# Two dense layers of a graph network in fp32: normalising a tile behind the product, the residual sum on VectorE, and the third layer's first transposes ahead of the second's last products

## What is computed

```python
h = (1.0 + eps) * node_feats + aggr                      # acc, 10 tiles of 128x512
h = gelu(layer_norm(h @ W1 + b1, g1, be1))               # W1 512x1024, layer 1
h = gelu(layer_norm(h @ W2 + b2, g2, be2))               # W2 1024x512, layer 2
h = layer_norm(node_feats + h, gA, bA)                   # layer A
m = gelu(h @ M1) @ M2                                    # M1 512x1024, M2 1024x512
return x + layer_norm(h + m, gB, bB)                     # layer B
```

## Time and profile before

| | before |
|---|---|
| median of 3 runs | 560.19 us (559.36 to 563.92) |
| the profiled execution | 567.65 us, of which span 565.8 us |
| busy share of the span: PE, DVE, ACT, POOL | 84%, 72%, 53%, 57% |
| chain that ended last: PE, DVE, issue, ACT, POOL | 43%, 23%, 15%, 7%, 6% |
| edges, W1, W2, M1 with M2 begin at about | 0, 302, 371, 443 us |

### The profile page before, as it was taken

How to read it: one execution, slowest core, us unless ns; L and a number is a source line. 1 busy time by engine, 2 the same in 40 slices (tenths; PEclk the granted TensorE clock), 3 DMA queues, 4 the chain that set the end, 5 groups by cost and what they waited for, 6 DMA issues and landing times.

```text
span 565.8 us, 7924 instructions
## 1 busy us (share of the span) xinstructions
PE 476.6 (84%) x1915; PEld 351.2 (62%) x1916; DVE 407.6 (72%) x550; ACT 300.2 (53%) x569; POOL 325.2 (57%) x306
## 2 busy tenths in 40 slices
PE   1072999977989897998868999999999699999994
PEld 0041666643656564665546887778877589888883
DVE  7861999872968686878891788878999844572465
ACT  3741786871876776878881444456554466004000
POOL 4675788875788787878730444426777542240152
PEclk9997799996989898999987999999999799999998
DMA  7676677776667676679306422343442031121022
GB/s 277 236 229 204 173 216 216 216 215 191 194 193 218 195 222 198 209 217 321 112 1 206 167 74 74 131 149 107 149 149 72 8 93 57 38 74 39 20 93 74
DMA packets 34296, 85.26 MB, mean 151 GB/s; under 512 B 4912, under 2 KB 5248, under 8 KB 34240
## 3 DMA queue, kind: packets, MB, share of 16 engines
q0 software_dynamic: 12560, 41.17, 25.1%
q1 hardware_dynamic: 20864, 42.74, 22.4%
q10 hardware_dynamic: 816, 0.77, 0.5%
HBM read 72.07 MB, written 5.24 MB: 137 GB/s over the span
## 4 chain that ended last, share of the span: by engine, by line
PE 43%; DVE 23%; issue 15%; ACT 7%; POOL 6%; ACTq 2%; DMA 2%; another core or an unknown queue 1%; DVEq 1%; POOLq 0%
PE ps_t L1154 7%; PE ps_u L1128 5%; PE ps_u L1138 5%; PE ps_u L1129 5%; PE ps_u L1130 5%; DVE work L1021 5%; PE ps_t L1130 4%; PE ps_t L1128 4%; PE ps_t L1129 4%; DVE msg_lo L952 3%; DVE z L947 3%; POOL rstd L533 3%; POOL rows L520 2%; ACT squares L754 2%; PE ps_t L1138 2%
## 5 line engine op out<-in xcount | busy, mean ns | idle before, releaser
L520 POOL DMA_INDIRECT rows<-gather_table,src_idx x157 | 191.1, 1217 | 61.5 <-issue 43.3
L696 ACT ACTIVATE msg_hi<-z 128x1024 fp32r<-128x1024 f32 (+1 forms) x79 | 82.7, 1047 | 61.0 <-DVE z L947 43.0
L952 DVE SCALAR_TENSOR_TENSOR msg_lo<-z,msg_hi 128x1024 fp32r<-128x1024 f32 (+1 forms) x79 | 100.9, 1279 | 0.7 <-ACT msg_hi L696 0.7
L1138 PE MATMUL ps_u<-we_raw,attr_raw 128*128 128x512 f32 x104 | 58.9, 651 | 42.3 <-DVE attr_lo L958 38.6
L947 DVE TENSOR_TENSOR z<-ps_u,rows 128x1024 f32<-128x1024 f32 (+1 forms) x53 | 64.1, 1210 | 38.9 <-remote 18.2
L531 POOL TENSOR_TENSOR var_eps<-mv,eps_t 128x1 f32<-128x1 f32 x40 | 11.5, 287 | 135.9 <-DVE mv L1009 68.3
L1128 PE MATMUL ps_u<-w_hi,lhs_lo 128*128 128x512 f32 x160 | 65.9, 412 | 4.2 <-DVE lhs_lo L1000 3.0
L1130 PE MATMUL ps_u<-w_hi,lhs_hi 128*128 128x512 f32 x160 | 63.8, 399 | 0.0
L1129 PE MATMUL ps_u<-w_lo,lhs_hi 128*128 128x512 f32 x160 | 63.8, 399 | 0.0
L1154 PE MATMUL ps_t<-msg_lo,onehot 128*128 128x512 f32 x145 | 60.6, 418 | 0.9 <-issue 0.9
L1154 PE MATMUL ps_t<-msg_hi,onehot 128*128 128x512 f32 x145 | 58.0, 400 | 0.0
(11 more groups left out here) (158 smaller groups left out, 1059.7 us busy)
## 6 DMA issues: line engine op xcount, KB each, us to landing
attr_raw<-in_attr_t SPq DMA_DIRECT2D x40, 256.0 KB
w_raw<-in_W SPq DMA_DIRECT2D x24, 256.0 KB, 2.7
tile_in<-mid SPq DMA_DIRECT2D x10, 512.0 KB, 3.3
res<-in_x SPq DMA_DIRECT2D x20, 256.0 KB, 2.7
xin<-in_x SPq DMA_DIRECT2D x5, 512.0 KB, 7.2
gather_table<-tab SPq DMA_DIRECT2D x5, 512.0 KB, 2.8
out<-work SPq DMA_DIRECT2D x10, 256.0 KB, 2.0
rows<-gather_table,src_idx POOLq DMA_INDIRECT x157
```

Of the source, the lines that this page charges most:

```text
L520: g.indirect_dma_start(rows[:, group.r, e % TPG, :], None, gather_table[:, :], bass.IndirectOffsetOnAxis(src_idx[:, e:e + 1].bitcast(u32), ...
L696: a.activation(pair(msg_hi, g, p), summed(g, p), ACT.Relu).then_inc(msg_hi_done, 1)
L952: v.scalar_tensor_tensor(pair(msg_lo, g, p), summed(g, p), 0.0, pair(msg_hi, g, p).bitcast(f32), ALU.max, ALU.subtract).then_inc(msg_lo_do ...
L1138: t.matmul(o[:, D:2 * D], attr_raw[:, g.k, (2 * p + 1) * P:(2 * p + 2) * P], we_raw[:, :], start=True, stop=True)
```

## The change

It touches the dense stages alone.

- Normalising is moved back by a tile: in `after(i)` VectorE and ScalarE now do layer 1's or 2's normalising and Gelu for tile i - 1, and layer A's normalising for tile i - 2.
- Layer A's residual sum moves from GpSimd (`add_input`) to VectorE (`add_residual`), where it also gives the row sum, so VectorE's `bn_stats` and `bn_aggr` of layer A go away; the variance of layer A is a new `squares` on ScalarE. The semaphore `res_added`, on which SyncE waits, is now raised by VectorE.
- In W2, ScalarE makes `w_hi` of the chunk at the head of its work for a tile, ahead of `lhs_hi`. GpSimd's `w_lo` waits until the normalising of tile i - 1 is done.
- `turn(2, 0)` and `turn(2, 1)` now stand ahead of the products of tiles 8 and 9 of W2, not both behind tile 8's; VectorE's and ScalarE's parts of them move with them.

```diff
--- before.py
+++ after.py
@@ -273,7 +273,7 @@
-        LN = {k: {n: sem(f"ln{k}_{n}") for n in (("mean", "squared", "done") if k in "12" else ("stats", "moments")) +
+        LN = {k: {n: sem(f"ln{k}_{n}") for n in (("mean", "squared", "done") if k in "12A" else ("stats", "moments")) +
...
@@ -527,39 +527,40 @@
             def weight_low(s, i, p):
+                if s < 2 and not zero(i):
+                    pool.wait_ge(LN["12"[s]]["done"], i)
...
-            def add_input(s, i, p):
-                if s == 1:
-                    pool.wait_ge(gelu2_ready, i + 1)
-                    g.tensor_tensor(work[p][:, D:H], work[p][:, D:H], res[p][:, :], ALU.add).then_inc(res_added, 1)
+            def shift_input(i, p):
...
+            def after(s, i, p):
+                weights = not (isinstance(i, int) and i >= CHUNKS)
+                if s == 0:
+                    inv_std("1", i, p)
+                    if weights:
+                        weight_low(0, i, p)
+                elif s == 1:
+                    if not zero(i, 1):
+                        inv_std("A", i - 2, 2 + p)
+                    if weights:
+                        weight_low(1, i, p)
+                    inv_std("2", i, p)
...
-            def after(s, i, p):
-                if s < 2:
-                    inv_std("12"[s], i, p)
-                    if s == 1:
-                        if not zero(i):
-                            inv_std("A", i - 1, 3 - p)
-                        add_input(s, i, p)
-                    if not (isinstance(i, int) and i >= CHUNKS):
-                        weight_low(s, i, p)
...
@@ -748,30 +750,55 @@
-            def variance(ln, i, p, width):
+            def variance(ln, i, slot, x, width):
                 act.wait_ge(LN[ln]["mean"], i + 1)
-                a.activation(squares[:, 0:width], work[p][:, 0:width], ACT.Square, bias=neg_shift[:, p:p + 1],
-                             scale=float(width) ** -0.5, accum_out=mv[:, p, 1:2]).then_inc(LN[ln]["squared"], 1)
+                if not zero(i):
+                    act.wait_ge(LN[ln]["squared"], i)
+                elif ln != "1":
+                    act.wait_ge(LN["1"]["squared"], NT)
+                first = D if ln == "A" else 0
+                a.activation(squares[:, first:first + width], x, ACT.Square, bias=neg_shift[:, slot:slot + 1],
+                             scale=float(width) ** -0.5, accum_out=mv[:, slot, 1:2]).then_inc(LN[ln]["squared"], 1)
...
+            def gelu2(i, p):
+                act.wait_ge(LN["2"]["done"], i + 1)
+                a.activation(work[p][:, D:H], work[p][:, 0:D], ACT.Gelu).then_inc(gelu2_ready, 1)
...
             def after(s, i, p):
                 s2, i2 = ahead(s, i, p)
-                lhs_high(s2, i2, p)
-                variance("12"[s], i, p, H if s == 0 else D)
-                if not (isinstance(i, int) and i >= CHUNKS):
+                weights = not (isinstance(i, int) and i >= CHUNKS)
+                if s == 1 and weights:
                     weight_high(s, i, p)
+                if s2 < 2 or i2 == 0:
+                    lhs_high(s2, i2, p)
+                variance("12"[s], i, p, work[p][:, 0:H if s == 0 else D], H if s == 0 else D)
+                if s2 == 2 and i2 == 0:
+                    lhs_high(2, 1, 1)
                 if s == 0:
-                    act.wait_ge(LN["1"]["done"], i + 1)
-                    a.activation(tile(mid, i), work[p][:, :], ACT.Gelu).then_inc(up_ready, 1)
+                    if weights:
+                        weight_high(s, i, p)
+                    if not zero(i):
+                        gelu1(i - 1, 1 - p)
                 else:
-                    if isinstance(i, int):
-                        act.wait_ge(res_in[p], 16 * (i // 2 + 1))
+                    input_rows(i, p)
+                    if zero(i):
+                        gelu1(NT - 1, 1)
                     else:
-                        act.wait_ge(res_in[p], 8 * (i - p) + 16)
-                    a.activation(res[p][:, :], res[p][:, :], ACT.Relu, bias=x_nbias[:, ds(i, 1)], scale=x_rstd[:, ds(i, 1)])
-                    act.wait_ge(LN["2"]["done"], i + 1)
-                    a.activation(work[p][:, D:H], work[p][:, 0:D], ACT.Gelu).then_inc(gelu2_ready, 1)
+                        gelu2(i - 1, 1 - p)
+                        variance("A", i - 1, 3 - p, work[1 - p][:, D:H], D)
@@ -797,7 +824,9 @@
                         after(s, 2 * j + p, p)
                 for p in range(2):
                     after(s, NT - 2 + p, p)
+            gelu2(NT - 1, 1)
             lhs_high(2, 2, 0)
+            variance("A", NT - 1, 3, work[1][:, D:H], D)
             inner_parts(act, 0, inner_values)
             lhs_high(2, 3, 1)
@@ -1020,56 +1049,71 @@
+            def add_residual(i, p):
                 x = work[p][:, D:H]
-                if part == 0:
-                    dve.wait_ge(res_added, i + 1)
-                    moments("A", i, 2 + p, x, D)
-                else:
-                    normalize("A", i, 2 + p, x, gA, bA, tile(acc, i)).then_inc(h_ready, 1)
+                dve.wait_ge(gelu2_ready, i + 1)
+                v.scalar_tensor_tensor(x, x, 1.0, res[p][:, :], ALU.mult, ALU.add, accum_out=total[:, 2 + p:3 + p]).then_inc(res_added, 1)
+                dve.wait_ge(res_added, i + 1)
+                mean("A", 2 + p, D)
...
             def after(s, i, p):
-                x = work[p][:, 0:D]
                 s2, i2 = ahead(s, i, p)
-                if s2 == 2 and i2 == 1:
-                    lhs_low(s2, i2, p)
                 if s == 0:
                     if zero(i):
                         dve.wait_ge(vec1_in["b1"], 16)
                     if not zero(i, 1):
                         dve.wait_ge(up_ready, i - 1)
                     add_product(s, i, p, b1[:, :], H)
+                    if not zero(i):
+                        norm1(i - 1, 1 - p)
+                    lhs_low(s2, i2, p)
                 else:
                     if zero(i, 1):
                         dve.wait_ge(up_ready, NT - 1 + i)
                     else:
                         dve.wait_ge(gelu2_ready, i - 1)
                     add_product(s, i, p, b2[:, :], D)
-                if not (s2 == 2 and i2 == 1):
-                    lhs_low(s2, i2, p)
-                if s == 0:
+                    if s2 == 2 and i2 == 0:
+                        lhs_low(2, 0, 0)
                     if zero(i):
-                        for name in ("g1", "be1"):
-                            dve.wait_ge(vec1_in[name], 16)
-                    normalize("1", i, p, work[p][:, :], g1, be1, work[p][:, :]).then_inc(LN["1"]["done"], 1)
-                else:
+                        norm1(NT - 1, 1)
+                    else:
+                        norm2(i - 1, 1 - p)
+                    if s2 < 2:
+                        lhs_low(s2, i2, p)
+                    elif i2 == 0:
+                        lhs_low(2, 1, 1)
+                    if not zero(i, 1):
+                        norm_a(i - 2, p)
                     if not zero(i):
-                        layer_a(i - 1, 1 - p, 0)
-                    normalize("2", i, p, x, g2, be2, x).then_inc(LN["2"]["done"], 1)
-                    if not zero(i):
-                        layer_a(i - 1, 1 - p, 1)
+                        add_residual(i - 1, 1 - p)
@@ -1106,9 +1150,11 @@
-            for part in range(2):
-                layer_a(NT - 1, 1, part)
+            norm2(NT - 1, 1)
+            norm_a(NT - 2, 0)
             lhs_low(2, 2, 0)
+            add_residual(NT - 1, 1)
+            norm_a(NT - 1, 1)
@@ -1273,13 +1319,12 @@
                 last.then_inc(product_done, 1)
             def step(s, i, p):
+                s2, i2 = ahead(s, i, p)
+                if s2 == 2:
+                    turn(2, i2, p)
                 product(s, i, p)
-                s2, i2 = ahead(s, i, p)
                 if s2 < 2:
                     turn(s2, i2, p)
-                elif i2 == 0:
-                    turn(2, 0, 0)
-                    turn(2, 1, 1)
             def inner(b, f, k):
```

50 lines of the change are left out of this document (35 added, 15 removed).

## The result

| | before | after |
|---|---|---|
| median | 563.52 us (559.36 to 568.56, 19 runs) | 565.41 us (562.12 to 570.96, 19 runs) |
| ratio after / before | | 1.0047, 95% interval 1.0025 to 1.0068 |
| span of the profiled execution | 565.8 us | 569.2 us |
| first turn of W1, M1's first product | 301.58, 443.44 us | 303.28, 443.91 us |
| chain that ended last: PE, DVE, issue, DMA, POOL, ACT | 43%, 23%, 15%, 2%, 6%, 7% | 47%, 15%, 14%, 7%, 5%, 5% |

The account below looks back on a forecast made before the run. VectorE was taken to set W1's and W2's pace, TensorE close behind. W1's 3.4 us gain precedes W2's load loop; block 7 ends as before (0), low clock adds 1.7: 560.2 + 1.7 = 561.9 us, range 556.5 to 567.

Parts of the forecast that it names:

- W1: W1: VectorE stops waiting, needs under 5.7 us a tile, TensorE sets the pace; W2's first product 3.4 us earlier.
- The loop in W2: W2: residual sum releases `res`, then `w_raw`, `w_hi`, `lhs_hi`, `lhs_lo`, normalising A, next residual sum: 8.6 us a tile.
- The loop's own price: W2: a loop round takes 8.6 us a tile, where before it was 7.05 and TensorE needs 6.3.
- Rival 1: W2: loads keep their lead, TensorE sets the pace; 12 us less, 548 us; chance 0.11, half-way forms included.
- Rivals 2 and 3: W2: crowding loads land 1.1 us later, 568 us, 0.14; SBUF passes meet, up to 1.0 a tile, 567 us, 0.07.
- rival 2: W2: `res`, `w_raw` and `tile_in` loads crowd, 1.1 us more a round, 568 us; decides from landing 3.5; chance 0.14.
- Block 4: M1: TensorE needs `ff_hi` of block 0 at 453.4, waits 3.8 us for ScalarE's late Gelu, starts at 457.2.
- VectorE's tail: End of W2 into M1: VectorE's last-tile work, with 0.4 wait for ScalarE, ends at 455.2; ScalarE's variance follows to 456.0.
- The low clock: M1, behind the wait at block 4: clock 0.72 over 6 us, costing 1.7 us.
- After block 7 both kernels run the same, TensorE without a wait.: M1 after block 7 to the end: no difference between the kernels and no wait of TensorE.
- The sum: Whole kernel: block 7 ends as before, plus the low clock: 0 + 1.7 = +1.7 us, giving 561.9 us.
- TensorE's wait "about 2 us a tile": W2's second half: a sign of the forecast, TensorE waiting about 2 us a tile.

Follow-up runs that it names:

- experiments 1, 2 and 4: On the changed kernel, in W2: weight load ahead of `res` load (0.9833); `w_hi` copy at ScalarE's tile end (0.9898); residual sum ahead of A's normalising (0.9972).
- Experiment 1: Changed kernel with W2's weight chunk load issued ahead of the residual rows' load on SyncE: 553.42 us, ratio 0.9833 to before.
- experiment 7: Changed kernel with M2's weight chunks 0 and 1 loaded ahead of the residual rows of tiles 8 and 9: ratio 1.0022 to before.
- experiment 8: Changed kernel with W2's weight loads and M2's first two ahead of residual rows' loads, M1's blocks 0 and 1 activations ahead of A's last variance: 0.9809 to before.
- experiment 10: experiment 8 plus VectorE's splits of M1's blocks 0, 1 ahead of A's last normalising, GpSimd's M2 `w_lo` 0, 1 ahead of its last inverse deviation: 541.52 us, 0.9737.

## Why the prediction was right

Times of after are given less 1.70 us here, so that both kernels' W1 starts together.

- **W1.** Right. The third turn of 8 transposes comes at 373.2 where it came at 376.65, 3.4 us earlier as forecast; W2's first product starts at 367.7 (369.37 less 1.70), as forecast. VectorE's passes, to be held against the earlier trace rows:

```profile
332.10 1.23 DVE L1059 SCALAR_TENSOR_TENSOR work<-ps_u,b 128x1024 f32<-128x1024 f32 x1 [1.45 <-PE ps_u L1176]
...
333.50 1.28 DVE L1044 SCALAR_TENSOR_TENSOR work<-work,neg_mean,g 128x1024 f32<-128x1024 f32 x1
334.81 1.28 DVE L1050 SCALAR_TENSOR_TENSOR work<-work,rstd,be 128x1024 f32<-128x1024 f32 x1
```

  The second pass takes 1.28 us where it took 2.24, and the only wait is for TensorE.
- **The loop in W2.** Right, term by term. Residual sum and issue 0.90 (forecast 0.99), from `res` to `w_raw` 0.54 (0.55), landing and wake-up 2.93 (2.8), the rest 4.29 (4.28): 8.66 for 8.6. Chunk 2's copy starts at 388.0 (388.0), chunk 7's at 431.2 (431.1), and M1 at 442.2 (442.3). The experiments 1, 2 and 4 show the loop; it was argued before them.
- **The loop's own price.** Right. Rival 1 put an open loop 12 us under before. Experiment 1, which opens it, is 11.2 us under before in the sum of the parts, and 9.4 us (6.8 to 12.0) by its ratio.
- **Rivals 2 and 3.** Neither came. Landing in W2 was 2.8 to 2.9 us, where rival 2 needs 3.5, and the passes of normalising A in the round above take 0.74 and 0.75 us, so nothing meets them.
- **Block 4.** The mechanism is right, the size was off. TensorE came to block 4 at 453.45 (453.4) but waited 3.00 us, not 3.8. The mis-sized term is mainly VectorE's tail: the wait of 0.4 us for ScalarE ahead of `ff_in_lo` of turn 2 did not come, and the work around it was about 0.2 us shorter, so ScalarE's variance began at 454.6 and not at 455.2. From there to block 4 it was 1.8 us, not 2.0.

```profile
458.15 0.80 PE L1174 MATMUL ps_u<-ff_in_hi,w_lo 128*128 128x512 f32 x1 [3.00 <-ACT ff_hi L813]
```

- **The low clock.** Right: behind that wait the granted clock is 0.72 over 6 us, which costs the 1.7 us that were put down for it. Block 7 ends at 469.1 with that cost in it, where 468.3 and 1.7 were forecast: 0.9 us earlier.
- **"After block 7 both kernels run the same, TensorE without a wait."** This step failed. From block 7's end after takes 98.36 us and before 97.52, 0.8 us more. One wait of 0.64 us at 479.0 (not shifted) is in it, for ScalarE's `ff_hi`; the other 0.2 us are open. ScalarE had been held up at M2's chunks, for which it waited 5.8 us in three waits, and 0.4 us in before:

```profile
463.29 0.63 ACT L751 ACTIVATE w_hi<-w_raw 128x512 fp32r<-128x512 f32 x1 [1.16 <-DMA w_raw<-in_W]
...
468.34 0.63 ACT L751 ACTIVATE w_hi<-w_raw 128x512 fp32r<-128x512 f32 x1 [1.74 <-DMA w_raw<-in_W]
...
474.44 0.63 ACT L751 ACTIVATE w_hi<-w_raw 128x512 fp32r<-128x512 f32 x1 [2.89 <-DMA w_raw<-in_W]
```

  I had followed the late residual sum into W2's loads and into ScalarE's tail, and not into the chunks that ScalarE copies between M1's blocks: each chunk's load waits for the subtraction of the chunk two before it, so a late first copy makes all of them late. ScalarE has no idle time between the copy at 474.44 and that `ff_hi`. Loading the first two earlier does not help (experiment 7), nor do earlier copies alone (experiment 8, 1.58 us). In experiment 10 `w_lo` of chunk 0 starts 9.8 us behind M1's start, where experiment 8 has 13.3 and after 14.9, and the wait is 0.5 us.
- **The sum.** From the first turn of W1 to the end (569.15 and 565.83 us), after takes 265.87 us and before 264.25, so 1.6 us more where 1.7 was forecast. That this is so near is luck: -0.9 up to block 7 and +0.8 behind it are two errors of opposite sign. What is left open is how much of the measured 2.6 us (1.4 to 3.8) is more than that. The forecast of 561.9 us lies 3.5 under the measured median; 3.3 of it is before's own, 560.19 in three runs and 563.52 in 19.
- **Signs and sums.** TensorE's wait "about 2 us a tile" in W2's second half came in two rounds only (2.1 and 1.8 us, of two waits each); behind each of them the low clock took its place. Two sums of the prediction are off by 0.2 us, and nothing rests on it: ten products and turns from 367.7 end at 430.9 and not 431.1, and the last product of W2 at 439.4 and not 439.6.

## What to carry to other kernels

When a sum or a reduction moves to a later place on another engine, list what waits for its semaphore, queue by queue: here a DMA queue carried the delay to a load that had nothing to do with the sum, and its user stood ahead of the work that makes the next sum. Such a loop puts the whole landing into each round, however idle the engines are; here one swap of two issues gave the load a round more, and the loop no longer bound. And at a seam between stages look at every in-order queue for work of the old stage ahead of the new stage's first blocks: here one queue alone only moved the wait, two made it longer, and all four together took it away.
